# Per-tile values and one matmul per head in place of a weighted sum of normalised context rows

## The reference

```python
lat = layernorm(latents, ln_l_w, ln_l_b)          # 128 x 256
ctx = layernorm(context, ln_c_w, ln_c_b)          # 12544 x 256
q = (lat @ Wq), k, v = split(ctx @ Wkv)           # heads of 64, inner width 1024
attn = softmax(clip(q k^T * 64**-0.5, -11, 11))   # per head, 128 x 12544
x = x + (attn @ v) @ Wo + bo
x = x + self_attention(layernorm(x))              # 16 heads of 16, LoRA on q, k, v, o
x = x + fp8_linear(layernorm(x))
```

## Time and profile before

| | |
|---|---|
| median of 3 | 1160.64 us |
| the profiled execution | 1157.79 us |
| its span, first to last instruction | 1156.1 us |
| TensorE matmuls busy | 1137.3 us (98%) |
| TensorE weight loads busy | 936.4 us (81%) |
| DVE busy | 829.5 us (72%) |
| ACT busy | 598.8 us (52%) |
| GpSimd busy | 309.0 us (27%) |
| mean granted TensorE clock | 0.986 |

### The profile page before, as it was taken

The page is one execution under the profiler, slowest core; times in us unless marked ns, Lnnn a source line. Parts: engine busy times, 40 slices in busy tenths (PEclk is TensorE's granted clock), DMA queues, the critical chain, the costliest instruction groups (busy, mean ns, idle before and its releaser), DMA issues.

```text
span 1156.1 us, 18331 instructions
## 1 busy us (share of the span) xinstructions
PE 1137.3 (98%) x5056; PEld 936.4 (81%) x5056; DVE 829.5 (72%) x1622; ACT 598.8 (52%) x1029; POOL 309.0 (27%) x516
## 2 busy tenths in 40 slices
PE   6999999999999999999999999999999999999997
PEld 5888888888888888888888888888888888888774
DVE  5778778777777777787776776776766766766624
ACT  4555555555555555555555555555555555555411
POOL 5334334334334233242221221221211211211100
PEclk8999999999999999999999999999999999999996
DMA  5221221221211211354212212212112112110000
GB/s 178 69 69 46 68 68 45 68 63 51 68 61 53 68 55 59 108 108 81 74 46 69 67 46 68 62 51 68 57 56 68 53 61 68 51 64 24 1 1 5
DMA packets 81393, 70.72 MB, mean 61 GB/s; under 512 B 40115, under 2 KB 67670, under 8 KB 81366
## 3 DMA queue, kind: packets, MB, share of 16 engines
q1 hardware_dynamic: 80390, 68.94, 20.1%
q10 hardware_dynamic: 976, 1.45, 0.4%
HBM read 70.13 MB, written 0.13 MB: 61 GB/s over the span
## 4 chain that ended last, share of the span: by engine, by line
PE 96%; issue 2%; DMA 1%; DVE 1%; POOL 0%; ACT 0%; SPq 0%; POOLq 0%; DVEq 0%; ACTq 0%
PE bank L466 31%; PE bank L467 31%; PE bank L468 31%; PE bank L511 1%; DMA wkT<-in_WkT_dram 1%; PE bank L572 1%; PE bank L584 1%; PE bank L503 0%; PE bank L614 0%; PE bank L596 0%; PE bank L630 0%; PE bank L594 0%; POOL wkT L457 0%; DVE fold_y L909 0%; PE bank L604 0%
## 5 line engine op out<-in xcount | busy, mean ns | idle before, releaser
L732 ACT ACTIVATE ex<-bank,c_rstd 128x512 f32<-128x512 f32 x392 | 270.1, 689 | 242.4 <-PE bank L468 166.4
L403 POOL TENSOR_TENSOR z_lo<-z,z_hi 128x255 fp32r<-128x255 f32 x196 | 174.9, 892 | 742.1 <-ACT z_hi L745 742.1
L739 ACT CAST p_hi<-ex 128x512 fp32r<-128x512 f32 x392 | 243.8, 622 | 240.8 <-DVE ex L899 148.6
L903 DVE TENSOR_TENSOR p_lo<-ex,p_hi 128x512 fp32r<-128x512 f32 x392 | 271.6, 693 | 116.3 <-ACT p_hi L739 99.7
L466 PE MATMUL bank<-qk_hi,d_hi 128*128 128x512 f32 x784 | 305.9, 390 | 0.0
L467 PE MATMUL bank<-qk_lo,d_hi 128*128 128x512 f32 x784 | 305.5, 390 | 0.0
L466 PE MATMUL bank<-p_hi,z_hi 128*128 128x512 f32 x784 | 305.5, 390 | 0.0
L468 PE MATMUL bank<-p_hi,z_lo 128*128 128x512 f32 x784 | 305.5, 390 | 0.0
L468 PE MATMUL bank<-qk_hi,d_lo 128*128 128x512 f32 x784 | 305.3, 389 | 0.0
L467 PE MATMUL bank<-p_lo,z_hi 128*128 128x512 f32 x784 | 305.2, 389 | 0.0
L899 DVE TENSOR_SCALAR ex<-ex 128x512 f32<-128x512 f32 x392 | 189.8, 484 | 156.5 <-ACT ex L732 154.6
(11 more groups left out here) (162 smaller groups left out, 410.0 us busy)
## 6 DMA issues: line engine op xcount, KB each, us to landing
t_all<-in_ctxT_dram SPq DMA_DIRECT2D x98, 384.0 KB, 3.2
x_pair<-in_ctx_dram SPq DMA_DIRECT2D x98, 256.0 KB, 2.7
diff<-sig_all SPq DMA_DIRECT2D x194, 0.5 KB, 1.9
wq<-in_Wq_dram ACTq DMA_DIRECT2D x2, 512.0 KB, 6.9
wkT<-in_WkT_dram SPq DMA_DIRECT2D x2, 512.0 KB, 6.1
wv<-in_Wv_dram SPq DMA_DIRECT2D x1, 1024.0 KB
wo<-in_Wo_dram SPq DMA_DIRECT2D x1, 1024.0 KB
crow_all<-in_crows_dram ACTq DMA_DIRECT2D x1, 256.0 KB, 7.6
```

The lines of the kernel that those rows point to most:

```text
L403: pool.tensor_tensor(z_lo[s][:, b, 0:LAST], z[s][:, b, 0:LAST], z_hi[s][:, b, 0:LAST].bitcast(F32), ALU.subtract).then_inc(s_zlo, 1)
L732: act.activation(ex[c][:, :], sc_bank[c][:, :], ACT.Exp, scale=c_rstd[s4][:, b:b + 1])\
L739: act.copy(p_hi[b][c][:, :], ex[c][:, :]).then_inc(s_phi, 1)
L903: dve.tensor_tensor(p_lo[b][c][:, :], ex[c][:, :], p_hi[b][c][:, :].bitcast(F32), ALU.subtract)\
```

## The change

The normalised rows z are gone. For every tile and pass TensorE now computes the values themselves, 128 keys x 512 (8 heads of 64), from the same `d_hi`/`d_lo` as the scores and from folded value weights split into `wv_hi`/`wv_lo`: 6 matmuls of 512 columns into one bank, `v_bank`. ACT scales them by the inverse deviation and rounds them to the high part, DVE makes the low part, and both stand side by side in `vhl` (64 high, 64 low columns per head). The probabilities' parts stand side by side as well, `ph` (128 x 2 x 512). The weighted sum is then one matmul per head: 128 weight columns (high and low values) and 256 moving columns (high and low probabilities), 8 per tile. It holds four products per head, which are added on saving (`save`).

The denominators no longer come out of TensorE: the clipped exponentials are added up, those of chunk 0 by DVE and those of chunk 1 by POOL, and a matmul with ones adds them over the partitions once per pass and chunk. The outputs of a head stand transposed, so the transposes before Wo fall away; `reciprocal` now runs over 512 columns, four times.

`difference` moves from DVE to POOL for all pairs, `d_hi` from DVE to ACT, the row loads fall away in pass 1, mean and its copies too. The key weights are folded by matmuls (`key_fold`), with ten matmuls on the identity ahead (`keep_warm`). Work for the second pass and the outputs of the first hang on the written-out pairs of both passes, into one bank (`side_bank`).

```diff
@@ tensor
+            def values(p, gp, s, b, first=False):
+                g = 2 * gp + b
+                if b == 0:
+                    pe.wait_ge(s_dlo, gp + 1)
+                if not first:
+                    pe.wait_ge(s_vlo, g)
+                keys, cols = slice(b * P, (b + 1) * P), slice(p * IH, (p + 1) * IH)
+                for k in range(KD):
+                    ins = mm3(v_bank[:, :], d_hi[s][:, k, keys], d_lo[s][:, k, keys], wv_hi[:, k, cols], wv_lo[:, k, cols],
+                              k == 0, k == KD - 1)
+                ins.then_inc(s_v, 1)
...
-            def weighted_sum(gp, s, b, c, start, stop, saved=0):
+            def weighted_sum(gp, b, c, start, stop, saved=0):
                 g = 2 * gp + b
                 pe.wait_ge(s_plo, CH * g + c + 1)
                 if c == 0:
-                    pe.wait_ge(s_zlo, g + 1)
+                    pe.wait_ge(s_vlo, g + 1)
                 if saved:
                     pe.wait_ge(s_save[c], saved)
+                for m in CHUNK_M[c]:
+                    for a in range(2):
+                        at = a * CM + m % CM
+                        ins = pe.matmul(acc[m][:, a, :, :], vhl[b][:, 2 * m + a, :, :].rearrange("p n d -> p (n d)"),
+                                        ph[b][c][:, :, at * P:(at + 1) * P], start=start and a == 0,
+                                        stop=stop and a == 1)
+                ins.then_inc(s_pv, 1)
-                for k in range(KD):
-                    ks = slice(k * P, (k + 1) * P)
-                    ins = mm3(acc[k][c][:, :], z_hi[s][:, b, ks], z_lo[s][:, b, ks], p_hi[b][c][:, :], p_lo[b][c][:, :],
-                              start, stop)
-                ins.then_inc(s_pv, 1)
...
                     for c in range(CH):
                         if not ended:
                             scores(next_p, gp + b, slot(p, phase, b, 2), 1 - b, c)
-                        weighted_sum(gp, slot(p, phase, 0, 2), b, c, first, last, saved=p * KD if first else 0)
+                        weighted_sum(gp, b, c, first, last, saved=p * CM if first else 0)
@@ gpsimd
+            def add_den(p, g, first=False):
+                pool.wait_ge(s_clip, CH * g + 2)
+                if first:
+                    pool.tensor_copy(den[p][1], ex[1][:, :]).then_inc(s_den[1], 1)
+                else:
+                    pool.wait_ge(s_den[1], g)
+                    pool.tensor_tensor(den[p][1], den[p][1], ex[1][:, :], ALU.add).then_inc(s_den[1], 1)
...
             def pair(p, i, phase):
                 gp = p * PAIRS + i
+                add_den(p, 2 * gp + 1)
+                beside(p, i, phase)
+                add_den(p, 2 * gp + 2)
@@ scalar, pair: for b in range(2)
+                    if more1:
+                        v_high(g + 1, s4, 1 - b, used=not (begun and b == 0))
                     for c in range(CH):
                         if more1:
                             exps(g + 1, s4, 1 - b, c)
                             p_high(g + 1, 1 - b, c, used=not (begun and b == 0))
+                        if (b, c) == (1, 0) and not (ended and i + 2 >= PAIRS):
+                            act.copy(d_hi[s2][:, :, :], diff[s2][:, :, :]).then_inc(s_dhi, 1)
@@ scalar, exps
                 if not first:
                     act.wait_ge(s_plo, CH * (g - 1) + c + 1)
+                    act.wait_ge(s_den[c], g)
@@ vector
+            def v_low(g, s4, b):
+                dve.wait_ge(s_vhi, g + 1)
+                dve.scalar_tensor_tensor(vhl[b][:, :, 1, :], v_bank[:, :].rearrange("p (h d) -> p h d", h=HP),
+                                         c_rstd[s4][:, b:b + 1], vhl[b][:, :, 0, :].bitcast(F32), ALU.mult, ALU.subtract)\
+                   .then_inc(s_vlo, 1)
@@ vector, pair: for b in range(2)
+                    clip(g + 1, 0)
+                    v_low(g + 1, s4, 1 - b)
+                    p_low(g + 1, 1 - b, 0)
+                    if b == 0 and new_stats:
+                        ctx_stats(gp + 3, landed(p, i, phase, 3, SLOTS), s3_4, 0)
+                    clip(g + 1, 1)
+                    if b == 0 and new_stats:
+                        ctx_stats(gp + 3, landed(p, i, phase, 3, SLOTS), s3_4, 1)
+                    add_den(next_p, g + 1, 0, first=next_p > p)
+                    if b == 1 and not (ended and i + 2 >= PAIRS):
+                        d_low(gp + 2, slot(p, phase, 2, 2))
+                    p_low(g + 1, 1 - b, 1)
+                    if b == 0 and new_stats:
+                        ctx_aggr(s3, 0)
+                        ctx_aggr(s3, 1)
+                        ctx_veps(gp + 3, s3)
...
+            def save(p, c):
+                dve.wait_ge(s_pv, CH * (TILES * (p + 1) - 1) + c + 1)
+                for m in CHUNK_M[c]:
+                    dve.tensor_reduce(osum[p][c][:, :, m % CM, :], acc[m].rearrange("p a n q -> p a q n"), AX_X, ALU.add)\
+                       .then_inc(s_save[c], 1)
+            def inverse(n, src):
+                dve.wait_ge(s_denp, n + 1)
+                dve.reciprocal(rden[n % CH][:, :], src[:, :]).then_inc(s_rden, 1)
```

More of the change, by code:

```diff
@@ L537, in _ @@
                 scores(0, 0, 0, 0, c, first=True)
+            pe.wait_ge(s_wv[0], 16)
+            for k in range(KD):
+                value_fold(0, k, bank[k])
+            pe.wait_ge(s_wq[1], 16)
+            q_heads(1, range(MH), side_bank)
+            pe.wait_ge(s_wvlo, KD)
+            values(0, 0, 0, 0, first=True)
+            pe.wait_ge(s_qT, CH + 1)
             def pair(p, i, phase):
@@ L546, in pair @@
                     ended = last and p == PASSES - 1
+                    if next_p > p and not ended:
+                        pe.wait_ge(s_wvlo, KD * PASSES)
+                        pe.wait_ge(s_qklo, 2 * KD * CH)
+                    if not ended:
+                        values(next_p, gp + b, slot(p, phase, b, 2), 1 - b)
                     for c in range(CH):
@@ L769, in _ @@
                 exps(0, 0, 0, c, first=True)
+            for c in range(CH):
+                wv_high(c, 0, c, bank[c])
                 p_high(0, 0, c, used=False)
+            qT_scaled(CH, MH, range(MH), side_bank)
+            v_high(0, 0, 0, used=False)
+            d_high(1)
             def pair(p, i, phase):
@@ L774, in pair @@
                 static = isinstance(i, int)
-                over = static and i == PAIRS - 1
-                ended = over and p == PASSES - 1
+                ended = static and p == PASSES - 1
+                begun = static and p == 0 and i == 0
                 for b in range(2):
                     g = 2 * gp + b
-                    more1 = not (ended and b == 1)
-                    start = static and p == 0 and i == 0
+                    more1 = not (ended and i == PAIRS - 1 and b == 1)
+                    s4 = slot(p, phase, b, SLOTS)
@@ L788, in pair @@
                         if more1:
-                            exps(g + 1, slot(p, phase, b, SLOTS), 1 - b, c)
-                            p_high(g + 1, 1 - b, c, used=not (start and b == 0))
-                        if c != b and not ended:
-                            z_high(gp + 1, slot(p, phase, 1, 2), b, used=not start)
-                if static and p == 0 and i in FOLD_PAIRS:
-                    centre(MH + FOLD_PAIRS.index(i))
-                if static and p == 0 and i in QK_PAIRS:
-                    for a in range(CH):
-                        qk_high(KD * CH + CH * QK_PAIRS.index(i) + a, 1, QK_PAIRS.index(i), a, bank[6 + a])
@@ L964, in pair @@
                 static = isinstance(i, int)
-                start = static and p == 0 and i == 0
                 ended = static and p == PASSES - 1
-                more = [not (ended and i + n >= PAIRS) for n in range(4)]
+                over = static and i == PAIRS - 1
                 new_stats = p == 0 and not (static and i + 3 >= PAIRS)
@@ L1037, in save_chunk1 @@
[L1037 to L1049 removed]
+                    more1 = not (ended and over and b == 1)
@@ L1051, in fp8_weights @@
+            for c in range(CH):
+                if c:
+                    save(1, c)
+                inverse(CH + c, DEN_BANK[c])
+                normalised(1, c)
             def fp8_weights():
```

740 lines of the change are left out of this document (372 added, 368 removed).

## The result

The changed kernel takes **1215.81 us** (median of 4 runs, 1214.24 to 1216.09), the kernel before 1161.39 on the same chip (4 runs, 1160.17 to 1162.51): ratio **1.0466** [1.0448, 1.0484], slower. The forecast was 1206.5 with a range of 1115 to 1235. The profiled execution took 1215.72 us, its span is 1214.0, the granted clock 0.987.

The account below looks back on a forecast made before the run. TensorE bounds the kernel before; after, POOL's wide operations hold up DVE's chain. Stream start 30.7 + stream 1101.5 + hung-in steps 18 + tail 51.8 = span 1202.0, as a median 1206.5 us, range 1115 to 1235.

Parts of the forecast that it names:

- the signs that it named: Marks of a right forecast: TensorE idle before values, DVE over 90% busy, 5.4 us per tile in pass 1, 5.8 to 5.9 in pass 0.
- TensorE's tile: TensorE's work per 128 keys: 18 matmuls at 0.227 plus 8 of 256 columns at 0.12, 5.04 us, 0.40 less.
- The weight-load rival: Weight loads set the pace of the 256-column matmuls: 1227 us at 0.19 each, 1256 at 0.227; chance 0.07.
- The hold: Time POOL's 512-column operations keep DVE off: 0.92 us for the addition, 0.97 for the difference, bounds 0.85 to 1.0.
- The walk: Step-by-step timing of one pair of tiles: 10.78 us in pass 1, 11.81 in pass 0, stream 1101.5 us.
- pass 1 first step: Pair's first tile in pass 1, clip of chunk 0 to next clip, with POOL's addition and difference: 5.34 us.
- Second step: Pair's second tile in pass 1, d_hi on ACT between p_hi and chunk 1's exponential: 5.44 us.
- Head: Everything before the stream of tiles: weights, key folds, scores, value fold, second queries; stream starts at 30.7 us.
- Hung-in steps: Extra work hung into the stream, such as subtractions, inversions, projection and saving: 18 us, bounds 11 and 24.
- Tail: From the stream's end to the kernel's end, with inversions, reductions and last projection: 51.8 us, 61.2 before.
- TensorE stays the bound: Rival: POOL's operations find DVE idle or barely delay it, so TensorE's 5.04 us per tile decides: 1097 us; chance 0.15.
- Only the additions collide: Rival: POOL's difference falls into idle DVE time, pairs 10.84 and 10.35 us, kernel 1138 us; chance 0.16.

Follow-up runs that it names:

- e9: Changed kernel with both additions and the difference on DVE, the difference in the pair's second step, ACT's d_hi behind chunk 1's exponential: 1103.63 us.
- e12: Changed kernel with POOL adding only 256 of the 512 columns of chunk 1's denominators per tile: 1138.59 us.
- e4: Changed kernel with only the difference moved from POOL to DVE, behind p_low of the pair's first step: 1176.81 us.
- e1: Changed kernel with POOL adding only 2 of the 512 columns of chunk 1's denominators per tile, all waits kept: 1116.94 us.
- e6: Changed kernel with both additions on DVE and POOL's difference held back until v_low of the pair's first step: 1151.99 us.
- e10: Changed kernel with both additions and the difference on DVE, and ACT's d_hi moved behind the exponential of chunk 1: 1123.17 us.
- e11: Changed kernel with both additions and the difference on DVE, the difference in the pair's second step, d_hi not moved: 1136.83 us.
- e3: Changed kernel with only chunk 1's addition moved from POOL to DVE, the difference staying on POOL: 1174.37 us.

## Why the prediction held, step by step

The direction and the mechanism held; its 1206.5 was 9.3 us short. In the spans it is 12.0, 1214.0 against 1202.0: the forecast put 4.5 us between span and median, and 1.8 were measured. Of the signs that it named, a tile takes 5.50 in pass 1 and 5.97 in pass 0, for 5.4 and 5.8 to 5.9.

- **TensorE's tile**: 5.04 forecast; e9 runs at 10.16 a pair, 5.08. The four short matmuls at 304.25 are followed by the next wide one at 304.72: 0.117 each (0.12). The weight-load rival is refuted.

```profile
304.25 0.64 PE L528 MATMUL wide<-ph,vhl 128*128 128x256 f32 x4
...
304.72 0.40 PE L488 MATMUL wide<-qk_hi,d_hi 128*128 128x512 f32 x1
```

- **The hold** is the mis-sized term: 0.92 and 0.97 forecast, bounds 0.85 to 1.0, measured 1.09, outside them, for addition and difference alike. It was scaled from 255 columns on one clip, and the hold of that clip was read too small: 0.46, counted from 309.75, 0.12 behind z_lo's start. The excess of the durations is 0.97 - 0.43 = 0.54, and for d_hi, which takes 0.42 undisturbed (308.91), 0.96 - 0.42 = 0.54 too; 256 columns held for 0.54 in e12. From 0.54 on 255 columns the same scaling gives 1.08 for 512: the rows of before had the right hold in them. The difference's 0.97 was counted from the end of d_lo's record, though, as the walk has it, a 512-column operation frees its follower 0.08 earlier.
- **The walk**: pass 1 first step 5.34 forecast, 5.55 measured (clip of chunk 1 0.08 later, holds of 1.08 and 1.11 in place of 0.92 and 0.97, and the addition and p_low each free the next after 0.61 and not 0.69: +0.08 + 0.16 + 0.14 - 0.16 = 0.22). Second step 5.44 forecast, 5.45 measured: there the shorter addition and a clip 0.06 earlier cancel the hold. Pairs 10.78 and 11.81 forecast, 11.00 and 11.94 measured: 48.5 x 0.22 + 49 x 0.13 = 17.0 us.
- **Head**: stream start at 27.32, forecast 30.7: -3.4. The scores began at 15.87, not 21.
- **Hung-in steps**: from 27.32 to the stream's end at 1160.35 it is 1133.0; less 49 x 11.94 and 48.5 x 11.00 that leaves 14.4, forecast 18: -3.6.
- **Tail**: 53.7, forecast 51.8: +1.9. Nearly all of it is the last projection: eight matmuls of 256 columns take 3.60 where the eight at 1166.45 take 1.99. TensorE had waited 2.83 us for the inversion, and its granted clock in that stretch is 0.53, the level of 1.2 GHz, against 1.00 at 1166.45. The forecast had 1.8, without a drop of the clock. The reciprocals of 512 elements (forecast 3.4) came out right.

```profile
1161.95 3.36 DVE L1127 RECIPROCAL rden<-wide 128x512 f32<-128x512 f32 x1 [0.93 <-PE wide L698]
...
1166.45 1.99 PE L676 MATMUL wide<-wkv,osum 128*128 128x256 f32 x8
...
1167.15 3.35 DVE L1127 RECIPROCAL rden<-wide 128x512 f32<-128x512 f32 x1
...
1171.28 3.60 PE L676 MATMUL wide<-wkv,osum 128*128 128x256 f32 x8 [2.83 <-DVE osum L1133]
```

17.0 - 3.4 - 3.6 + 1.9 = 11.9 of the 12.0. So 7 us of errors of the other sign in the head and the hung-in steps, and 2.7 between span and median, hid part of the walk's error: that the sum came within 9.3 us is partly luck.

- **The rivals**: *TensorE stays the bound* asked that POOL find DVE idle. In this order it doesn't, but e9, where nothing wide is left on POOL, shows its price: 1103.6 where 1097 was worked out. *Only the additions collide* was wrong for this kernel: the difference took 1.08 of p_low in pass 0 and 0.61 of the clip in pass 1, and e4 gained 39 us by moving it. (In pass 1 of e1, where the additions no longer collide, its hold costs nothing.)
- **Unforeseen**: in pass 0 ACT's exponential of chunk 0 waits for DVE's held addition (30.4 us over 42 times). In the pair shown it costs nothing: the exponential of 310.31 ends at 311.00, and the clip that needs it starts at 312.20, behind DVE's own work.

The Trainium skill (SBUF — State Buffer, "Who interferes with whom") has the lock held for the full instruction. The runs differ from it, as the trace of before did: the difference that takes 1.29 without a wait of its own held p_low for 1.11 (e6), additions of 256 columns, which take 0.74 without a wait (407.20 of e12), held d_low for 0.54, and a power of 0.69 held p_low not at all (301.20).

## What to carry to other kernels

- An operation given to GpSimd isn't free when it and DVE's work, both on SBUF operands, exclude one another: price it at what it withholds from DVE (here 1.09 us for 512 columns) and compare with DVE doing it itself (0.61). Here DVE was the cheaper place for all of it, though it was the busier engine.
- Ask what each step of a repeating pair has idle, not what the pair has: e10 and e11 each failed where both edits together gave 21 us.
- An operation in a queue also holds back what stands behind it. Taking POOL's addition out moved its difference onto the worst place, at 0.85 us of the clip a pair (e3).

## What the runs showed of the hardware

- The hold grows with the width: 0.54 us for 256 columns, 1.09 to 1.11 for 512, nothing to be seen for two (e1's additions of two columns leave d_low its 0.69, though they wait for DVE's addition themselves: 0.58 at 303.29 against 0.20 at 308.29).
- A wide GpSimd operation that waits while DVE works gets the next turn, before the DVE operation queued behind (302.98; 402.25 of e12). Its own span then reads 1.67 instead of 1.30, wait included.
- Matmuls of 256 columns with a 128x128 load each run at 0.117 us, half of a 512-column one's 0.23, though a load is shown at 189 ns.
